# A graph network on Trainium2: windows of 128 nodes put in order of their number of edge tiles

## The chip, the cores and the metric

The kernel runs on one core of one Trainium2 chip. The metric is the device time of one execution in microseconds; the time shown is the median of 3 runs. The input is 6,250 nodes of 256 features and 100,000 edges sorted by destination; the destinations are drawn as 6250 u², so the first nodes have many edges and the last ones few.

## The reference

```python
x = layernorm(x + gcn(x, L0_W, edges))            # out[dst] += (x @ W)[src] * deg_inv_sqrt[src] * deg_inv_sqrt[dst]
y = x
for l in range(3):                                # 8 heads of 32
    Q, K, V = typed(y, W_Q[l]), typed(y, W_K[l]), typed(y, W_V[l])      # one of 4 matrices, by the node's type
    kt = typed(K[src], W_E[l], edge_type)                               # one of 3, by the edge's type
    s = sum(Q[dst] * kt, -1) / sqrt(32) * mu[l].T[edge_type]
    w = softmax of s over the edges with the same dst
    agg = segment_sum(V[src] * w, dst)
    y = layernorm(y + agg @ Wo[l] + bo[l]) * g1 + b1
    y = layernorm(y + gelu(y @ w1 + c1) @ w2 + c2) * g2 + b2
return layernorm(x + layernorm(y) * out_g + out_b)
```

## The kernel before

The nodes lie in `WINDOWS` = 50 windows of 128 (48 whole ones, window 48 with 106 nodes, window 49 empty). The edges of a window are cut into tiles of 128, and each window has at least one tile; a fixed `NT` = 832 tiles are worked on, two at a time (a duo), 16 tiles in a block. Tiles follow the windows in their order 0, 1, 2, ... The program is a row of stages, each a block of instructions for the five engines, with a barrier of all engines behind it (`end_phase`, L88), so that nothing of one stage runs beside another.

- `constants` (L137): masks, and the type of each node as a one-hot, `g.type_hot`. The types are loaded with one window in a row, turned by TensorE (L165), copied (L200) and compared (L203).
- `index_tiles` (L208): finds where each window's edges end (L450 to L462), the number of tiles of each window (`TILED`, L467), and by a running sum the tile at which each window starts (L468). From that it makes the window of each tile (`window_hot`, L476), gathers the edges of the tiles (POOL, L347, 7 gathers), counts the degree of each node (L513 to L531, then L388: the counts of the tiles summed into windows), and writes the tables of register words that steer the edge stages (L577 to L659). SyncE meanwhile copies x to SBUF (L321), and to `x_d`, the node state in DRAM (L323). The rows of x times 1/sqrt(degree) go to `xs_d` (L328).
- `gcn_edges` (L688): POOL gathers two times 128 rows of `xs_d` per duo (L764); TensorE multiplies them with a one-hot of the destinations into one of 4 PSUM banks, clears the next bank and ScalarE copies the bank of the window before to `g.sums`, for every tile, whether its window ended or not (L803 to L834). Which bank and which row is a word read into a register: `load_words` (L99), 16 or 24 words at once, each fourth duo.
- `gcn_nodes` (L1070): for windows two at a time (25 steps): the sums are scaled (L1155), turned (L1123), multiplied with W (L1132), added to x in `y` (L1235) and normalised. SyncE loads x in five batches of ten windows (L1105), then the weights of the projection (`load_weights`, L1295: `pj_wk` four times, `pj_we`, `pj_mu`, then eight parts of `pj_w`). TensorE turns the weights right after step n = 8 (`WEIGHTS_TURNED`; `turn_weights`, L1329, waits for all six of `k_in`). The new rows go to `x_d` and `x1_d` (L1113).
- The projection (`Projection`, L1260): for each of 49 windows, POOL spreads the rows by type (L1410), TensorE turns (L1346) and multiplies them (L1356), ScalarE and VectorE copy values, keys and query rows out, and SyncE stores keys and values in `kv_table` (`store_all`, L1307: two DMAs per window, each window at rows 128 n).
- `attention_edges` (L1477), three times: as `gcn_edges`, with gathers of `kv_table` (L1621), scores, softmax and weighted sums; also steered by words. `attention_nodes` (L1895), three times: output projection, layer norms and the feed-forward part for two windows at a time, with the next layer's projection behind it, in the last layer the final norms and the store of the result (L1991, one DMA per step).

SyncE's work stands in the order in which the code lists it: a DMA behind a wait or behind another DMA is issued after it.

```python
                for k in range(BATCHES):
                    some = batch_of(k)
                    sp.dma_start(y[:, some[0]:some[-1] + 1], windows_in(g.x_d, some)).then_inc(x_in[k], 16)
                pj.load_weights(sp)
```

Of the kernel before, what the change touches and what calls it, by code (L numbers as in the profile page):

```python
# [15 lines left out]
P = 128  # L16
# [36 lines left out]

FIRST_ROW, ZERO_ROW, UNREAD_ROW = ROWS, ROWS + 2, ROWS + 3
# [50 lines left out]

SUM_TOP = (SUM_BANK + SUM_BANKS - 1) * 512
# [30 lines left out]
def constants(nc, g):  # L137

    with ExitStack() as ctx:
        diff = ctx.enter_context(nc.sbuf_tensor("diff", [P, P], I32))  # L140
        type_rows = ctx.enter_context(nc.sbuf_tensor("type_rows", [WINDOWS, P], I32))
        type_rows_f = ctx.enter_context(nc.sbuf_tensor("type_rows_f", [WINDOWS, P], F32))
        type_col = ctx.enter_context(nc.sbuf_tensor("type_col", [P, WINDOWS], F32))
# [4 lines left out]
        turned = ctx.enter_context(nc.semaphore("const_turned"))  # L148
        whole = N // P
        with nc.Block() as block:  # L150
# [9 lines left out]

            @block.tensor
            def _(t):
                t.wait_ge(made, 6)
                t.wait_ge(masks, 3)
                t.transpose(g.ps[:, 0, 0:WINDOWS], type_rows_f[:], g.ident[0:WINDOWS, 0:WINDOWS]).then_inc(turned, 1)  # L165
# [19 lines left out]
            def _(v):  # L185
# [12 lines left out]
                v.tensor_copy(type_rows_f[:], type_rows[:]).then_inc(masks, 1)  # L198
                v.wait_ge(turned, 1)
                v.tensor_copy(type_col[:], g.ps[:, 0, 0:WINDOWS]).then_inc(masks, 1)  # L200
                v.wait_ge(masks, 4)
                for k in range(NODE_TYPES):
                    v.tensor_scalar(g.type_hot[:, :, k], type_col[:], float(k), None, ALU.is_equal)  # L203

        end_phase(nc, [made, masks, cleared, loaded, turned])


def index_tiles(nc, g):  # L208

    with ExitStack() as ctx:  # L210
# [3 lines left out]
        def sem(name):  # L214
# [25 lines left out]
        work = sb("ix_work", [P, 12, WINDOWS])  # L240
        ints = sb("ix_ints", [P, WINDOWS], I32)
# [37 lines left out]
            sem("ix_end_spread"))  # L279
        vec, base_ready, wdiag_ready, wrow_spread, wrow_copied = (  # L280
# [11 lines left out]
        K_COL, END_AT, DEG_AT = slice(0, 1), slice(64, 64 + WINDOWS), slice(128, 128 + WINDOWS)  # L292
# [7 lines left out]
        with nc.Block() as block:  # L300

            @block.sync
            def _(sp):
# [19 lines left out]
                sp.dma_start(g.x_d[0:N, :], g.x).then_inc(stored, 16)  # L323
                sp.dma_start(g.x_d[N:N + P, :], g.zeros[:, 0:D]).then_inc(stored, 16)
                sp.dma_start(g.x_d[N + P:NPAD, :], g.zeros[0:NPAD - N - P, 0:D]).then_inc(stored, 16)
# [25 lines left out]
            def _(t):  # L351
# [2014 lines left out]
```

## Time and profile before

| | us |
|---|---|
| time, median of 3 runs (lowest, highest) | 7778.57 (7768.23, 7786.26) |
| span of the profiled execution, first to last instruction | 6558.3 |
| the median less that span | 1220.3 |
| `constants` and `index_tiles` | 0 to 188 |
| `gcn_edges` | 188 to 1278 |
| `gcn_nodes` and first projection | 1278 to 1513 |
| `attention_edges`, three times | 1142, 1143, 1134 |
| `attention_nodes` with projection, twice | 580, 586 |
| last `attention_nodes` | 460 |

The profiled execution's own time is not among what is shown, only its span; the runs' median is 1220.3 us above that span. The bounds of the stages are read from the timeline, to a microsecond or two. SPq, PEldq, ACTq and DVEq are the sequencers of SyncE, TensorE, ScalarE and VectorE: rows of theirs are DMA issues and register instructions, which do not count as busy.

### The profile page before, as it was taken

How to read it: one execution, taken by the hardware profiler on the slowest of the kernel's cores; microseconds unless marked ns; L12 is line 12 of the kernel's file. 1: busy time of each engine (PE TensorE's matmuls, PEld its weight loads, DVE VectorE, ACT ScalarE, POOL GpSimd, SP SyncE). 2: the span in 40 equal slices, each digit the busy share in tenths (PEclk: the TensorE clock that was granted, in tenths of full speed). 3: DMA queues.
4: the chain of work that ended last, by engine and by line, in shares of the span. 5: the costliest groups of instructions: out<-in, count | busy, mean ns of one | idle time of the engine just before them, and what ended most of it. 6: DMA issues, size and time to landing. Idle time of an engine off the chain costs nothing. (4 is left out here: it accounts for less than half of the span.)

```text
span 6558.3 us, 128194 instructions
## 1 busy us (share of the span) xinstructions
PE 5376.9 (82%) x28010; PEld 4214.7 (64%) x28011; DVE 4522.3 (69%) x11029; ACT 3285.2 (50%) x10707; POOL 4047.3 (62%) x3930
## 2 busy tenths in 40 slices
PE   4566666697888888999888888889997888888897
PEld 3344444496666666788766666668896666666786
DVE  7433333356888888666488888876656888888697
ACT  0333333454666666323466666652244666666443
POOL 0677777546777777233577777743356777777343
PEclk9999999998999999999999999999998999999998
DMA  4444444578777777112887777741168777777111
GB/s 137 123 141 141 140 138 142 154 262 256 233 237 234 234 235 234 31 32 79 275 254 239 234 235 238 236 137 32 32 209 266 236 236 233 238 239 234 38 48 42
DMA packets 574994, 1165.93 MB, mean 178 GB/s; under 512 B 86616, under 2 KB 334128, under 8 KB 574752
## 3 DMA queue, kind: packets, MB, share of 16 engines
q0 software_dynamic: 239984, 774.78, 40.4%
q1 hardware_dynamic: 321359, 377.52, 17.5%
q10 hardware_dynamic: 13536, 12.33, 0.6%
q8 instruction: 44, 0.72, 0.0%
q14 instruction: 71, 0.57, 0.0%
HBM read 966.73 MB, written 204.00 MB: 179 GB/s over the span
## 5 line engine op out<-in xcount | busy, mean ns | idle before, releaser
L1621 POOL DMA_INDIRECT at_kv<-kv_table,at_stage x1664 | 1656.4, 995 | 545.0 <-issue 403.5
L1637 ACT COPY sums<-ps x2499 | 949.8, 380 | 1141.6 <-PE ps L1733 1116.8
L1718 PE MATMUL ps<-at_wv,at_hot 128*128 128x264 f32 x3328 | 1026.7, 403 | 348.5 <-ACT at_hot L1654 194.4
L1621 POOL DMA_INDIRECT at_kv_last<-kv_table,at_stage_last x832 | 824.7, 991 | 273.1 <-issue 205.4
L764 POOL DMA_INDIRECT gc_rows<-x_scaled,gc_stage x832 | 807.4, 970 | 269.9 <-issue 238.3
L1718 PEld LDWEIGHTS ps<-at_wv,at_hot 128*128 128x128 f32 x3328 | 515.1, 191 | 613.7 <-DVE at_wv L1820 354.4
L1733 PE MATMUL ps<-sums,at_hot_t 128*128 x3328 | 873.7, 386 | 26.7 <-DVE at_prod L1802 20.9
L825 PE MATMUL ps<-gc_rows,gc_hot 128*128 128x256 f32 x1664 | 552.4, 428 | 287.3 <-DMA gc_rows<-x_scaled,gc_stage 286.8
L1802 DVE TENSOR_TENSOR at_prod<-ps,at_kv 128x512 f32<-128x512 f32 x832 | 571.5, 687 | 285.5 <-DMA at_kv<-kv_table,at_stage 265.3
L1701 PE MATMUL ps<-zeros_b 128*128 128x264 bf16 x2508 | 695.8, 278 | 32.5 <-PEq L93 19.0
L1733 PEld LDWEIGHTS ps<-sums,at_hot_t 128*128 128x128 f32 x3328 | 579.2, 194 | 188.5 <-issue 19.9
L1718 PE MATMUL ps<-at_wv_last,at_hot_last 128*128 128x264 f32 x1664 | 508.7, 401 | 172.3 <-ACT at_hot_last L1654 111.9
L778 ACT COPY sums<-ps x833 | 310.9, 373 | 665.4 <-PE ps L825 649.8
L913 DVE CAST gc_hot_t<-ps 128x256 uint8<-128x256 f32 x416 | 176.3, 424 | 669.2 <-PE ps L825 665.3
L1843 DVE TENSOR_REDUCE at_score<-at_prod 128x16 f32<-128x512 f32 x832 | 563.8, 678 | 0.6
L825 PEld LDWEIGHTS ps<-gc_rows,gc_hot 128*128 128x128 f32 x1664 | 271.0, 205 | 425.2 <-DMA gc_rows<-x_scaled,gc_stage 367.9
L1820 DVE TENSOR_TENSOR at_wv<-at_kv,at_weight 128x462 f32<-128x462 f32 x832 | 526.7, 633 | 18.5 <-ACT at_weight L1674 5.2
L1684 ACT ACTIVATE at_wv<-at_kv,at_weight 128x33 f32<-128x33 f32 x1664 | 449.7, 323 | 3.4
L1718 PEld LDWEIGHTS ps<-at_wv_last,at_hot_last 128*128 128x128 f32 x1664 | 257.5, 190 | 301.8 <-DVE at_wv_last L1820 140.7
L1733 PE MATMUL ps<-sums,at_hot_t_last 128*128 x1664 | 437.8, 387 | 13.5 <-DVE at_prod_last L1802 10.2
L1802 DVE TENSOR_TENSOR at_prod_last<-ps,at_kv_last 128x512 f32<-128x512 f32 x416 | 285.8, 687 | 126.4 <-DMA at_kv_last<-kv_table,at_stage_last 124.2
L1666 ACT CAST at_hot_t<-at_hot_t 128x256 f32<-128x256 uint8 x832 | 345.4, 416 | 37.0 <-PE ps L1733 37.0
(411 smaller groups left out, 10812.2 us busy)
## 6 DMA issues: line engine op xcount, KB each, us to landing
kv_table<-pj_v_next SPq DMA_DIRECT2D x98, 396.0 KB, 3.5
kv_table<-pj_k_next SPq DMA_DIRECT2D x98, 384.0 KB, 2.8
at_hot_t<-hot_columns SPq DMA_DIRECT2D x104, 256.0 KB, 4.2
at_kv<-kv_table,at_stage POOLq DMA_INDIRECT x1664, 3.8
at_hot<-hot_rows SPq DMA_DIRECT2D x104, 256.0 KB, 4.8
at_rec<-block_records SPq DMA_DIRECT2D x104, 226.0 KB, 4.1
kv_table<-pj_v SPq DMA_DIRECT2D x49, 396.0 KB, 3.2
kv_table<-pj_k SPq DMA_DIRECT2D x49, 384.0 KB, 2.6
```

The source lines that it names most:

```text
L764: nc.gpsimd.indirect_dma_start(rows[:, (2 * k + j) * D:(2 * k + j + 1) * D], None, g.xs_d, bass.IndirectOffsetOnAxis(index, 0)).then_inc(g ...
L825: mm = t.matmul(at[j], hot[:, k, j, :], rows[:, (2 * k + j) * D:(2 * k + j + 1) * D], start=False, stop=True, skip_group_check=True)
L1621: nc.gpsimd.indirect_dma_start(kv[:, 2 * k + j, :], None, g.tab_d.rearrange("t n c -> (t n) c"), bass.IndirectOffsetOnAxis(index, 0)).then ...
L1637: act.copy(dest, source).then_inc(evacuated, 1)
L1666: act.copy(hot_t[:, slot % HRING].rearrange("p j e -> p (j e)"), hot_t8[:, b, u, :]).then_inc(t_cast, 1)
L1684: d = act.activation(wv[:, slot % WRING, j, SPLIT * UHEAD:UROW], kv[:, 2 * slot + j, D + SPLIT * UHEAD:SLOT], ACT.Copy, scale=weight[:, pa ...
L1701: return t.matmul(bank, g.zeros_b[:, 0:P], g.zeros_b[:], start=True, stop=True, skip_group_check=True)
L1718: mm = t.matmul(own[j], hot[:, slot % HRING, j, :], wv[:, slot % WRING, j, :], start=False, stop=True, skip_group_check=True)
L1733: mm = t.matmul(ps[:, TRIO[slot], j * D:(j + 1) * D], hot_t[:, slot % HRING, j, :], q_rows[j], start=True, stop=True)
L1802: v.tensor_tensor(prod[:, slot % 2].rearrange("p (j c) -> p j c", j=2), ps[:, TRIO[slot], :].rearrange("p (j c) -> p j c", j=2), keys, ALU ...
L1820: v.tensor_tensor(wv[:, slot % WRING, :, 0:SPLIT * UHEAD].rearrange("p j (h e) -> p j h e", h=SPLIT), kv[:, 2 * slot:2 * slot + 2, D:D + S ...
L1843: v.tensor_reduce(score[:, par, 2 * w:2 * w + 2, :], prod[:, slot % 2].rearrange("p (j h e) -> p j h e", j=2, h=HEADS), AX.X, ALU.add).the ...
```

## The change

The 48 whole windows are ranked by their number of tiles, fewest first (equal numbers by window); window 48 and the empty one keep their places at the end. Everything that was at window w is now at its rank: tiles, sums, query rows, state in DRAM, types. Sources of edges are still real node numbers, so `kv_table`, `xs_d` and the result stay in the order of the nodes, and what moves between the two orders looks up the real row. `g.window_rows` (one partition, 50 int32) holds the row of the window of each rank.

- `index_tiles` makes the order: a key of 64 tiles + window, its diagonal and a sum over it (L494 and L495 of the changed kernel), comparison with all other keys and a sum (the rank), a one-hot of the rank; TensorE multiplies ones with four rows of values times that one-hot, and the types with the one-hot, and VectorE copies both back. A second one-hot, by real window, is made for the degrees, and the degrees are summed twice (14 matmuls for 7).
- `constants` no longer turns the types; the four comparisons are made in `index_tiles`.
- x goes to a new DRAM tensor `x_padded`, and `gcn_nodes` loads it window by window.
- `store_all` looks up the row of each window before its wait; the result is stored with one DMA per window.

The diff, cut to its core:

```diff
+RANKED = N // P
+ORDER_LAST = 60000.0
+assert RANKED == FILLED - 1 == WINDOWS - 2 and (E // P + WINDOWS) * 64 + WINDOWS < ORDER_LAST
...
+def window_row(nc, g, eng, at):
+
+    _, (row,) = nc.values_load_multi_w_load_instructions(
+        g.window_rows[0:1, bass.ds(at, 1)], [eng.engine], skip_runtime_bounds_check_because=IN_RANGE)
+    return nc.s_assert_within(row, 0, RANKED * P, skip_runtime_bounds_check_because=IN_RANGE)
...
-                t.transpose(g.ps[:, 0, 0:WINDOWS], type_rows_f[:], g.ident[0:WINDOWS, 0:WINDOWS]).then_inc(turned, 1)
-                v.tensor_copy(type_rows_f[:], type_rows[:]).then_inc(masks, 1)
-                v.tensor_copy(type_col[:], g.ps[:, 0, 0:WINDOWS]).then_inc(masks, 1)
...
-                sp.dma_start(g.x_d[0:N, :], g.x).then_inc(stored, 16)
+                sp.dma_start(g.x_pad[0:N, :], g.x).then_inc(stored, 16)
+                sp.dma_start(g.x_d[FILLED * P:NPAD, :], g.zeros[:, 0:D]).then_inc(stored, 16)
...
+                t.wait_ge(ranks_ready, 1)
+                t.matmul(ps[:, 0, RANKS_AT], g.ones[:], by_rank[:].rearrange("p a w -> p (a w)"), start=True, stop=True)
+                t.matmul(ps[:, 0, TYPES_AT], g.type_rows_f[:], ranked[0:WINDOWS, :], start=True, stop=True).then_inc(ranks_spread, 1)
...
-                for c in range(CHUNKS):
-                    mm = t.matmul(ps[:, 0, DEG_AT], deg_rows[:, c * P:(c + 1) * P], window_hot[:, c, :],
-                                  start=c == 0, stop=c == CHUNKS - 1)
+                for k, hots in enumerate((window_hot, real_window_hot)):
+                    for c in range(CHUNKS):
+                        mm = t.matmul(ps[:, 0, 128 + k * WINDOWS:128 + (k + 1) * WINDOWS], deg_rows[:, c * P:(c + 1) * P], hots[:, c, :],
+                                      start=c == 0, stop=c == CHUNKS - 1)
...
+                v.tensor_copy(work[:, WINDOW], g.iota[:, 0:WINDOWS])
+                then(v.scalar_tensor_tensor(out=work[:, ORDER, 0:RANKED], in0=work[:, TILED, 0:RANKED], scalar=64.0,
+                                            in1=g.iota[:, 0:RANKED], op0=ALU.mult, op1=ALU.add))
+                then(v.tensor_tensor(diagonal[:], work[:, 0:5], g.ident[:, None, 0:WINDOWS].to_broadcast([P, 5, WINDOWS]), ALU.mult))
+                then(v.tensor_reduce(cols[:], diagonal[:], AX.X, ALU.add))
+                then(v.tensor_scalar(smaller[:], work[:, ORDER], cols[:, ORDER:ORDER + 1], None, ALU.is_lt))
+                then(v.tensor_reduce(rank_col[:], smaller[:], AX.X, ALU.add))
+                then(v.tensor_scalar(ranked[:], g.iota[:, 0:WINDOWS], rank_col[:], None, ALU.is_equal))
+                v.tensor_tensor(by_rank[:], ranked[:, None, :].to_broadcast([P, 4, WINDOWS]),
+                                cols[:, 0:4, None].to_broadcast([P, 4, WINDOWS]), ALU.mult).then_inc(ranks_ready, 1)
+                v.wait_ge(ranks_spread, 1)
+                v.tensor_copy(type_col[:], ps[:, 0, TYPES_AT])
+                then(v.tensor_copy(work[:, 0:4].rearrange("p a w -> p (a w)"), ps[:, 0, RANKS_AT]))
+                v.tensor_scalar(g.window_rows[:], work[0:1, WINDOW], float(P), None, ALU.mult)
...
+                then(v.tensor_tensor(mask[:], window_hot[:], work[:, WINDOW, None, :].to_broadcast(shape), ALU.mult))
+                then(v.tensor_reduce(tv[:, PAST], mask[:], AX.X, ALU.add))
+                v.tensor_tensor(real_window_hot[:], g.iota[:, None, 0:WINDOWS].to_broadcast(shape),
+                                tv[:, PAST, :, None].to_broadcast(shape), ALU.is_equal)
...
+                for k in range(NODE_TYPES):
+                    v.tensor_scalar(g.type_hot[:, :, k], type_col[:], float(k), None, ALU.is_equal)
...
-                DEG, SAFE, ROOT, HALF = 7, 8, 9, 10
+                DEG, SAFE, ROOT, HALF = (slice(8 + 2 * k, 10 + 2 * k) for k in range(4))
...
-                    sp.dma_start(y[:, some[0]:some[-1] + 1], windows_in(g.x_d, some)).then_inc(x_in[k], 16)
+                    for at in some:
+                        sp.dma_start(y[:, at, :], g.x_pad[bass.ds(window_row(nc, g, sp, at), P), :]).then_inc(x_in[k], 16)
...
-                    v.wait_ge(x_in[n // PER_BATCH], 16)
+                    v.wait_ge(x_in[n // PER_BATCH], 16 * len(batch_of(n // PER_BATCH)))
...
+                row = window_row(self.nc, g, sp, n)
                 sp.wait_ge(self.out_k, n + 1)
-                rows = g.tab_d[:, bass.ds(P * n, P), :].rearrange("t p c -> p t c")
+                rows = g.tab_d[:, bass.ds(row, P), :].rearrange("t p c -> p t c")
...
-                            sp.dma_start(two_windows(g.out, n - 5), fin[:, 1 - b]).then_inc(stored[1 - b], 16)
+                            for w in range(2):
+                                row = whole_window_row(nc, g, sp, 2 * (n - 5) + w)
+                                sp.dma_start(g.out[bass.ds(row, P), :], fin[:, 1 - b, w, :]).then_inc(stored[1 - b], 16)
```

Of how the change moves instructions, three places. SyncE in `gcn_nodes`, before:

```order
L1102 DMA gn_w<-in_L_gnn_W 128x2x256
L1105 DMA gn_y<-x_state 128x10x256 x4
L1105 DMA gn_y<-x_state 128x9x256
L1298 DMA pj_wk<-in_L_gnn_W_K 32x8x32 x4
L1299 DMA pj_we<-in_L_gnn_W_E 32x24x32
L1300 DMA pj_mu<-in_L_gnn_mu 128x24
```

and in the changed kernel, the last of the loads of x and the weights (an ISA row is an instruction without a name of its own in this listing; here it stands for the arithmetic on the register):

```order
L119 TENSOR_LOAD window_rows
L1149 ISA
L1149 DMA gn_y<-x_padded 128x256
L1342 DMA pj_wk<-in_L_gnn_W_K 32x8x32 x4
L1343 DMA pj_we<-in_L_gnn_W_E 32x24x32
L1344 DMA pj_mu<-in_L_gnn_mu 128x24
```

The first three rows stand there 49 times in a row, behind `gn_w` and ahead of the weights, where there were five DMAs.

VectorE in `index_tiles`, between the number of tiles and the running sum over it (listed as SCALAR_TENSOR_TENSOR ix_work<-ix_work,zeros), before:

```order
L465 TENSOR_SCALAR ix_ints<-ix_work 128x50
L466 TENSOR_SCALAR ix_ints<-ix_ints 128x50
L467 TENSOR_SCALAR ix_work<-ix_ints 128x50
L468 SCALAR_TENSOR_TENSOR ix_work<-ix_work,zeros 128x50
L469 TENSOR_TENSOR ix_work<-ix_work 128x50
```

and in the changed kernel:

```order
L489 TENSOR_SCALAR ix_work<-ix_ints 128x50
L491 COPY ix_work<-iota 128x50
L492 SCALAR_TENSOR_TENSOR ix_work<-ix_work,iota 128x48
L494 TENSOR_TENSOR ix_diagonal<-ix_work,ident 128x250
L495 TENSOR_REDUCE ix_cols<-ix_diagonal 128x5
L496 TENSOR_SCALAR ix_smaller<-ix_work,ix_cols 128x50
L497 TENSOR_REDUCE ix_rank_col<-ix_smaller 128x1
L498 TENSOR_SCALAR ix_ranked<-iota,ix_rank_col 128x50
L499 TENSOR_TENSOR ix_by_rank<-ix_ranked,ix_cols 128x200
L502 COPY ix_type_col<-ps 128x50
L503 COPY ix_work<-ps 128x200
L504 TENSOR_SCALAR window_rows<-ix_work 1x50
```

Eleven instructions stand between L489 and the sum, with two matmuls on TensorE between L499 and L502.

SyncE in the loop of `store_all`, changed kernel:

```order
L119 TENSOR_LOAD window_rows
L1358 REGISTER_ALU
L1360 ISA
L1360 DMA kv_table<-pj_k 128x3x256
L1361 ISA
L1361 DMA kv_table<-pj_v 128x3x264
```

The load of the row is new there; the two DMAs and their address arithmetic were there before. On POOL and ScalarE no instruction is added or moved.

## Rows read from the trace of the kernel before

**Rows 1.** The page: span of the profiled execution

```profile
span 6558.3 us, 128194 instructions
```

**Rows 2.** Busy time by stage: GCN edges, attention edges of one layer

```profile
core 0: us, PE busy (x) PEld busy (x) DVE busy (x) ACT busy (x) POOL busy (x), PEclk, DMA share, GB/s
...
188.00:1278.00 1090.00, 714.67 (x3384) 467.74 (x3384) 403.07 (x1276) 398.18 (x1249) 813.04 (x858) 0.95 0.46 139
...
1513.00:2655.00 1142.00, 949.40 (x4632) 699.94 (x4632) 916.35 (x1925) 727.61 (x2602) 837.70 (x858) 0.98 0.77 231
```

**Rows 3.** Timeline (start us, us, queue, line, DMA, count): SyncE, start of the GCN nodes

```profile
1279.43 11.59 SPq L1105 DMA_DIRECT2D gn_y<-x_state  x5
1291.07 5.88 SPq L1298 DMA_DIRECT2D pj_wk<-in_L_gnn_W_K  x4
...
1299.14 2.42 SPq L1300 DMA_DIRECT2D pj_mu<-in_L_gnn_mu  x1
```

**Rows 4.** Waits in 1278 to 1372 us (us in total, times, longest)

```profile
PE ps L1332 <- DMA pj_mu<-in_L_gnn_mu: 2.2, 1, 2.2
```

**Rows 5.** Source line of all register loads (count: ns min/median/max, first, last)

```profile
L101 PEldq TENSOR_LOAD <-words x324: 1612/1618/1665, 1513.7 to 6089.1; - x162
...
L101 DVEq TENSOR_LOAD <-words x156: 523/530/775, 1576.6 to 6088.6; - x156
...
L101 PEldq TENSOR_LOAD <-gcn_words x104: 1102/1107/1943, 188.6 to 1263.4; - x104
```

**Rows 6.** Timeline 1420 to 1433 us, projection of one window

```profile
1421.36 0.37 SPq L1315 DMA_DIRECT2D kv_table<-pj_k  x1
1421.92 0.37 SPq L1316 DMA_DIRECT2D kv_table<-pj_v  x1
...
1422.14 1.04 PE L1346 MATMUL ps<-ident,pj_xm 128*128 128x128 f32 x8
...
1424.40 0.37 SPq L1315 DMA_DIRECT2D kv_table<-pj_k  x1
```

**Rows 7.** Timeline 2650 to 2662 us, the same weight loads on an empty queue

```profile
2657.85 1.88 SPq L1298 DMA_DIRECT2D pj_wk_next<-in_L_gnn_W_K  x4
...
2660.41 0.39 SPq L1300 DMA_DIRECT2D pj_mu_next<-in_L_gnn_mu  x1
```

**Rows 8.** Source line L1300 (pj_mu), issue to landing

```profile
DMA to landing us min/median/max: 2.6/2.6/4.6
```

**Rows 9.** Timeline 1312 to 1372 us, TensorE after 8 us without work

```profile
1353.31 1.94 PE L1346 MATMUL ps<-ident,pj_xm 128*128 128x128 f32 x8 [7.76 <-ACT pj_xmt L1386]
```

**Rows 10.** Timeline 0 to 210 us, the two places of the index work

```profile
4.97 0.18 PEld L165 LDWEIGHTS ps<-ident,type_rows_f 50*128 50x128 f32 x1 [4.62 <-issue]
...
5.59 0.50 DVE L203 TENSOR_SCALAR type_hot<-type_col 128x50 f32<-128x50 f32 x4
...
27.10 0.67 PE L357 MATMUL ps<-ix_end_diag,ones 128*128 128x50 f32 x2 [10.03 <-DVE ix_end_diag L457]
...
29.73 0.21 DVE L470 SCALAR_TENSOR_TENSOR ix_work<-ix_work 128x50 f32<-128x50 f32 x1
29.86 0.52 DVE L471 TENSOR_TENSOR ix_mask<-ix_work,ix_tile_iota 128x350 f32<-128x350 f32 x1
...
51.51 9.29 DVE L500 COPY_PREDICATED ix_listed<-ix_shift_bits,ix_listed 128x1337 f32<-128x1337 int32 x7 [12.95 <-DMA ix_listed<-edge_pack,ix_base_row]
```

**Rows 11.** Timeline 136 to 150 us, degrees of the windows

```profile
137.41 3.23 PE L388 MATMUL ps<-ix_window_hot,ix_deg_rows 128*128 128x50 f32 x14 [1.06 <-ACT ix_deg_rows L407]
```

**Rows 12.** Busy time by stretch (columns as rows 2), index gathers and after a wait

```profile
30.00:51.00 21.00, 3.35 (x14) 3.06 (x14) 8.12 (x36) 0.00 (x0) 6.76 (x7) 1.00 1.09 372
...
1346.00:1360.00 14.00, 6.69 (x40) 6.72 (x41) 6.85 (x26) 5.23 (x10) 4.22 (x3) 0.63 1.02 340
```

**Rows 13.** Timeline, last node stage, SyncE: store and load of one step

```profile
6464.97 0.37 SPq L1974 DMA_DIRECT2D an_x_last<-x_state  x1
```

**Rows 14.** Timeline, last node stage, POOL: use of what that step loads

```profile
6480.92 1.26 POOL L2161 TENSOR_TENSOR an_xb_last<-an_x_last,nw_rows_last 128x512 f32<-128x512 f32 x1
```

More of the change, by code:

```diff
@@ L197, in _ @@
                 v.wait_ge(loaded, 32)
-                v.tensor_copy(type_rows_f[:], type_rows[:]).then_inc(masks, 1)
-                v.wait_ge(turned, 1)
-                v.tensor_copy(type_col[:], g.ps[:, 0, 0:WINDOWS]).then_inc(masks, 1)
[L201 to L205, printed above, removed]
+                v.tensor_copy(g.type_rows_f[:], type_rows[:])
+        end_phase(nc, [made, masks, cleared, loaded])
 def index_tiles(nc, g):
@@ L239, in index_tiles @@
         end_diag = sb("ix_end_diag", [P, WINDOWS])
-        work = sb("ix_work", [P, 12, WINDOWS])
-        ints = sb("ix_ints", [P, WINDOWS], I32)
+        work = sb("ix_work", [P, 16, WINDOWS])
+        ints = sb("ix_ints", [P, 2, WINDOWS], I32)
+        diagonal = sb("ix_diagonal", [P, 5, WINDOWS])
+        cols = sb("ix_cols", [P, 5])
+        smaller = sb("ix_smaller", [P, WINDOWS])
+        rank_col = sb("ix_rank_col", [P, 1])
+        ranked = sb("ix_ranked", [P, WINDOWS])
+        by_rank = sb("ix_by_rank", [P, 4, WINDOWS])
+        type_col = sb("ix_type_col", [P, WINDOWS])
+        real_window_hot = sb("ix_real_window_hot", [P, CHUNKS, WINDOWS])
         mask = sb("ix_mask", [P, CHUNKS, WINDOWS])
@@ L458, in _ @@
                 v.wait_ge(end_spread, 1)
-                END, START, COUNT, TILED, TEND, TST, OFF = range(7)
+                END, START, COUNT, TILED, ORDER, TEND, TST, OFF = range(8)
+                WINDOW = COUNT
                 v.memset(work[:, START, 0:1], 0.0)
+                v.memset(work[:, ORDER, RANKED:RANKED + 1], ORDER_LAST)
+                v.memset(work[:, ORDER, RANKED + 1:WINDOWS], ORDER_LAST + 1.0)
                 then(v.tensor_copy(work[:, END], ps[:, 0, END_AT]))
@@ L464, in _ @@
                 then(v.tensor_tensor(work[:, COUNT], work[:, END], work[:, START], ALU.subtract))
[L465 to L467 removed]
+                then(v.tensor_scalar(ints[:, 0], work[:, COUNT], float(P - 1), None, ALU.add))
+                then(v.tensor_single_scalar(ints[:, 0], ints[:, 0], 7, ALU.arith_shift_right))
+                then(v.tensor_scalar(work[:, TILED], ints[:, 0], 1.0, None, ALU.max))
+                v.tensor_copy(work[:, WINDOW], g.iota[:, 0:WINDOWS])
[12 more added lines that the diff above has]
+                v.tensor_scalar(g.window_rows[:], work[0:1, WINDOW], float(P), None, ALU.mult)
                 then(v.tensor_tensor_scan(work[:, TEND], work[:, TILED], g.zeros[:, 0:WINDOWS], 0.0, ALU.add, ALU.add))
@@ L539, in _ @@
                                        op1=ALU.add).then_inc(kv_ready, 1)
-                DEG, SAFE, ROOT, HALF = 7, 8, 9, 10
+                DEG, SAFE, ROOT, HALF = (slice(8 + 2 * k, 10 + 2 * k) for k in range(4))
                 v.wait_ge(deg_ready, 1)
-                then(v.tensor_copy(work[:, DEG], ps[:, 0, DEG_AT]))
+                then(v.tensor_copy(work[:, DEG].rearrange("p a w -> p (a w)"), ps[:, 0, DEG_AT]))
                 then(v.tensor_scalar(work[:, SAFE], work[:, DEG], 1.0, None, ALU.max))
@@ L2003, in _ @@
                     pj.store_all(sp)
-                sp.wait_ge(stored[0], 16 * ((STEPS + 1) // 2))
-                sp.wait_ge(stored[1], 16 * (STEPS // 2))
+                each = 32 if last else 16
+                sp.wait_ge(stored[0], each * (STEPS // 2) + 16)
+                sp.wait_ge(stored[1], each * (STEPS // 2))
             @block.tensor
@@ L2094, in emit @@
                         act.wait_ge(scaled, JOINT * n)
-                        need(act, stored[1 - b], 16 * (i - 3 + b))
+                        need(act, stored[1 - b], 32 * (i - 3 + b))
                         for k in range(2):
@@ L2333, in gnn_kernel @@
                 nc.sbuf_tensor("idx_x", [P, NT], I32) as g.idx_x:
+            constants(nc, g)
             index_tiles(nc, g)
```

36 lines of the change are left out of this document (17 added, 19 removed).

## The prediction

> **What bounds the kernel now.** I read the table of stages first, to see where the time is and what it depends on. The four edge stages hold most of it: 1090 us for the GCN and 1142 us for the edges of one layer [rows 2], of which there are three. Their instructions come from loops over 416 duos, whatever window a tile belongs to: each tile is gathered, multiplied, cleared and copied out in the same way, and the table words alone say which bank and row. So a new order of the windows changes words, not work, and I carry these stages over unchanged. What is left are the stages in which instructions are added: index, GCN nodes, projection, and the last node stage.
>
> Next, the timeline of SyncE at the start of the GCN nodes. Five loads of x keep its queue for 11.59 us, the weights follow, and `pj_mu` is issued at 1299.14 [rows 3] and lands 4.6 us later [rows 8]. The list of waits shows that TensorE stood 2.2 us for just that load [rows 4], with its matmul at 1303.8, right behind step 8 of 25. So **SyncE's queue is already on the path there**: whatever is put ahead of the weights moves the rest of the stage.
>
> **The change part by part.** *Loads of x in the GCN nodes.* Five DMAs become 49 times a register load, address arithmetic and a DMA of 128 rows. No register load of SyncE is in the trace. Three kinds of others are [rows 5]: 24 words on TensorE's queue 1618 ns, 16 words there 1107 ns, 2 words on VectorE's 530 ns. The two of TensorE lie on a line of 64 ns per word, which gives 0.15 us for one word; the upper bound is the 1.11 us of 16 words. I take 0.53 us, the row nearest in the number of words. Behind it come arithmetic and DMA: in the projection the second DMA starts 0.56 us after the first (1421.36, 1421.92) [rows 6], which holds both. One turn is 0.53 + 0.56 = 1.09 us, 49 are 53.4 us, against 11.59 us before. The Trainium skill, page "DMA: Bandwidth & Descriptors", section "Latency and other measured facts", puts a floor of about 600 ns under such a load; by it the turn were 1.16 us and the sum 3.4 us higher, but the 530 ns of VectorE's row lie below that floor.
>
> Part of this comes back. Before, the weights' issues stood in a full queue (5.88 us for the first four) [rows 3]; on an empty one the first to `pj_mu` takes 2660.41 - 2657.85 = 2.56 us, landing 2.6 us later [rows 7, 8]. With 128 KB per 1.09 us the queue will be nearly empty. So the weights are there at 1279.43 + 53.4 + 2.56 + 2.6 = 1338.0 instead of 1303.7: **34.3 us later**. The first eight steps need only two batches of x (20 turns, 21.8 us, and a landing), so they are done long before, and TensorE, ScalarE and VectorE then all stand, as their queues are in order and step 9 is behind the turned weights on TensorE. What follows them is the same work as before, by which the 34.3 us reach the end of the stage whole. ScalarE has no backlog it could work off in that time: its normalisations are listed seven steps behind the turned columns that it then waits for. The stores of x and of the table are behind the weights as before.
>
> *TensorE's restart.* After 8 us without work eight transposes took 1.94 us [rows 9], against 1.04 us in the steady loop [rows 6], in a stretch with a granted clock of 0.63 [rows 12], between its two levels of 1.2 and 2.4 GHz. It will now stand for some 30 us in the middle of the stage; for that and the matmuls right behind I add 2 us.
>
> *Index stage.* Between the number of tiles and the running sum stand seven new instructions in a chain, then two matmuls, then two copies. Ones of 50 columns take 0.21 us and those of 350 take 0.52 us [rows 10], with some 0.03 us between: five small ones 1.2 us, two of 250 columns 0.9, one of 200 and the copy of 200 0.8. The matmul of 50 columns (two passes) took 0.67 us [rows 10]; one of 200 and one of 50, with the signals there and back, I put at 1.4 us. Sum 4.3 us. From `constants` go a transpose, a copy and the four comparisons (4.97 to 6.09) [rows 10], 1.1 us; the comparisons come again, with the three of 350 columns for the second one-hot, where VectorE stands 12.95 us for the gathers [rows 10], and so cost nothing (2.1 us if that cover were gone). The degrees: seven matmuls took 3.23 us and VectorE waited for them [rows 11]; seven more are 3.2 us. Fourteen chained instructions on 100 instead of 50 columns add 0.05 us each, 0.7 us. Index: 4.3 - 1.1 + 3.2 + 0.7 = **7.1 us**. The gathers that then start 3.2 us later run in a stretch where the DMA engines are fully busy (share 1.09) with x [rows 12], so they could lose up to some 5 us more, or nothing; I take nothing and keep 5 us for the range. One DMA of zeros more is issued there beside them, at no cost.
>
> *Stores of keys and values.* A window takes 3.04 us (1421.36 to 1424.40) [rows 6], of which SyncE issues for 0.93 us. The register load stands ahead of its wait, so 0.53 us fall into 2.1 us of waiting, 147 times at no cost. Only a load above 2 us would be felt.
>
> *The result.* One more DMA and two register loads per step of 17 us. Behind them is the load of x, issued at 6464.97 [rows 13], landed some 3 us later, and used at 6480.92 [rows 14]: it may be 12 us late. Nothing there. Ahead of the last store, of which the code is unchanged, all is done.
>
> Sum: 34.3 + 2 + 7.1 = **43.4 us**. The profiled execution's span is 6558.3 us [rows 1], the median 7778.57 us, 1220.3 us more. I take what lies around the span as unchanged, so the span becomes 6601.7 us and the time 7822 us, 0.56% more. A measurement of this kernel can tell about 0.2%, 15.6 us, from no change.
>
> **The rivals.**
>
> *A: the register load is dear on SyncE.* At 1.11 us, as for 16 words, a turn is 1.67 us, 49 are 81.8, the weights land at 1366.4, 62.7 us later; with 9.1 us for the rest +72, 7850 us. For it: each queue has its own price in [rows 5], and SyncE's is not among them. Against: two words cost half. The Trainium skill, "Runtime: NRT & Kernel Launch", in its table of the preamble, has 1.3 us for the loads of a few words, from DRAM; by it the time were 7860 us. Chance 0.14.
>
> *B: it is cheap.* At 0.15 us a turn is 0.71 us, 49 are 34.8, the weights land at 1319.4, 15.7 us later: +25, 7803 us. For it: TensorE's two rows. Against: VectorE's lies 0.3 us above the same line. Chance 0.12.
>
> *C: it is hidden.* If the queue reads the register while the DMA ahead of it is issued, a turn is the 0.56 us of a DMA alone; 27.4 us, weights at 1312.0, 8.3 us later. TensorE then hardly stands, and with 7.1 us of index work the sum is +15, 7794 us: not slower by what can be measured. It decides from a turn of 0.56 us down. Against: the same queue issues one instruction after the other in [rows 3]. Chance 0.07.
>
> *D: the order itself moves the edge stages,* by reads and writes of banks and rows that meet otherwise. They are 1090 and, with the other layers about as long as the one of [rows 2], some 3420 us, so 1% is 45 us: enough to take the whole loss back (7777 us) or to double it (7867 us). For it only that the gathers' landing is what VectorE and TensorE wait for; against it that the sources, and with them the addresses gathered, are the same set. Chance 0.03 up and 0.04 down, half of the latter to below the time before.
>
> **How the numbers follow.** The forecast has 0.60: 7822 us, by itself 7812 to 7832 with the 5 us of the gathers and the runs' own spread of 9 us. A 0.14, B 0.12, C 0.07, D 0.07. The range reaches from B less that spread to A, 7797 to 7853 us, and leaves out C and D. Faster by over 0.2%: half of D's way down, 0.02. Within 0.2%: C and the other half, 0.09. Slower: 0.89.
>
> **What would show it.** In the changed profile: SyncE's register loads near 0.53 us, and 49 loads of x in 50 to 57 us; a wait of TensorE for `pj_mu` of some 30 us instead of 2.2; index stage 7 us longer; projection still 3.05 us per window; edge stages within a few us of before. I am wrong if TensorE does not wait there, if the projection loop has a longer period, or if an edge stage moved by over 10 us.

## The result, and the profile after

| | before | changed |
|---|---|---|
| median, us | 7778.57 | 7812.52 |
| lowest to highest, us (11 runs each) | 7743.28 to 7799.5 | 7791.03 to 7844.16 |
| ratio, 95% interval | | 1.0049 [1.0033, 1.0065] |

The changed kernel is slower by 0.49%, 34 us (by the interval 26 to 51 us). It was forecast at 7822 us, 43.4 us more.

One thing first, without which the numbers can't be read: the same kernel before took 6550 to 6559 us on the two chips of the first eight experiments, and 7760 us on that of the last two. The profile shown of before is of the first kind, the profile after of the second. Page of the changed kernel:

```profile
span 7789.3 us, 128925 instructions
```

Its profiled execution took 7791.03 us, 1.7 us more than its span. So the 1220.3 us between span and median of before [rows 1] do not lie around the span: they are another speed of the same program. Where they are is seen in the busy time by stretch. GCN edges, changed kernel (columns as in rows 2):

```profile
208.00:1496.00 1288.00, 799.47 (x3384) 536.55 (x3384) 394.47 (x1276) 398.80 (x1249) 809.82 (x858) 0.79 0.40 118
```

The same 3384 matmuls and 858 POOL instructions as in [rows 2], but 1288 us instead of 1090, with granted clock 0.79 instead of 0.95 and 118 GB/s instead of 139. The change does not do this: the kernel before has it too on such a chip (experiment 9).

The index stage and the node stage, where the change adds work, can be compared directly. SyncE at the start of the GCN nodes, changed kernel (timeline; columns as in rows 3):

```profile
1496.67 0.40 SPq L1145 DMA_DIRECT2D gn_w<-in_L_gnn_W  x1
1497.81 39.83 SPq L1149 DMA_DIRECT2D gn_y<-x_padded  x49
1537.69 1.90 SPq L1342 DMA_DIRECT2D pj_wk<-in_L_gnn_W_K  x4
1539.64 0.44 SPq L1343 DMA_DIRECT2D pj_we<-in_L_gnn_W_E  x1
1540.13 0.52 SPq L1344 DMA_DIRECT2D pj_mu<-in_L_gnn_mu  x1
```

Against [rows 3]: the loads of x keep the queue for 39.83 us where it was 11.59, and the weights behind them are issued in 2.44 us on a queue that is by then nearly empty. All register loads of a row, changed kernel (source line; columns as in rows 5):

```profile
L119 SPq TENSOR_LOAD <-window_rows x196: 261/604/921, 1497.1 to 5843.3; - x196
```

The row mixes two kinds. The 49 loads ahead of the weights (the same line, 1497 to 1538 us) are the short ones:

```profile
L119 SPq TENSOR_LOAD <-window_rows x49: 261/269/507, 1497.1 to 1536.9; - x49
```

The 49 of each of the three projections have medians of 619, 670 and 701 ns. In the straight run the turns are 0.81 us apart (39.83 / 49), and with 0.27 us for the load some 0.54 us remain for arithmetic and DMA. Waits in the node stage, changed kernel:

```profile
PE ps L1377 <- DMA pj_mu<-in_L_gnn_mu: 23.7, 1, 23.7
ACT pj_wkt L1425 <- PE ps L1377: 22.5, 1, 22.5
DVE gn_y L1279 <- DMA gn_y<-x_padded: 15.9, 1, 15.9
```

TensorE waits 23.7 us for the last weight load, where it was 2.2 [rows 4], and ScalarE with it. VectorE's 15.9 us for the first ten windows of x are new too; they end before TensorE's wait does and cost nothing. TensorE on both sides of its wait (timeline):

```profile
1517.26 1.89 PE L1176 MATMUL ps<-gn_w,gn_at 128*128 128x256 f32 x8
1542.85 1.89 PE L1377 MATMUL ps<-ident,pj_wk 128*32 128x128 f32 x8 [23.70 <-DMA pj_mu<-in_L_gnn_mu]
1544.54 1.06 PE L1167 MATMUL ps<-ident,gn_a 128*128 128x128 f32 x4
1545.39 2.77 PE L1176 MATMUL ps<-gn_w,gn_at 128*128 128x256 f32 x8
1548.00 0.60 PE L1167 MATMUL ps<-ident,gn_a 128*128 128x128 f32 x4
```

and before:

```profile
1303.80 1.05 PE L1332 MATMUL ps<-ident,pj_wk 128*32 128x128 f32 x8 [2.25 <-DMA pj_mu<-in_L_gnn_mu]
1304.69 0.60 PE L1123 MATMUL ps<-ident,gn_a 128*128 128x128 f32 x4
1305.12 1.89 PE L1132 MATMUL ps<-gn_w,gn_at 128*128 128x256 f32 x8
```

The three groups behind the wait take 5.7 instead of 3.5 us: 2.2 us for the restart. The granted clock of these stretches:

```profile
1520.00:1543.00 23.00, 0.15 (x1) 0.13 (x2) 2.00 (x6) 2.28 (x6) 3.75 (x2) 0.57 0.57 151
1543.00:1550.00 7.00, 7.00 (x32) 5.79 (x30) 1.35 (x3) 4.63 (x10) 0.00 (x0) 0.70 0.16 25
1550.00:1560.00 10.00, 10.00 (x62) 8.80 (x61) 8.99 (x38) 8.11 (x19) 0.00 (x0) 1.00 0.38 125
```

While TensorE stands, the granted clock is 0.57, near the lower of its two levels (1.2 of 2.4 GHz); it is 0.70 in the stretch behind the wait and 1.00 in the next. The node stage closes to a tenth with these numbers. From the issue of `gn_w` to TensorE's restart it was 1303.80 - 1279.0 = 24.8 us and is 1542.85 - 1496.7 = 46.2, so 21.4 us more; with 2.2 for the restart 23.6. From `gn_w` to the first store of keys it was 81.2 us (1279.0 to 1360.2), and is 104.9 (1496.7 to 1601.6): 23.7 us more.

Index stage, changed kernel, VectorE from the number of tiles to the running sum, and the gathers (timeline, columns as in rows 10):

```profile
27.60 0.19 DVE L489 TENSOR_SCALAR ix_work<-ix_ints 128x50 f32<-128x50 int32 x1
...
31.96 0.21 DVE L502 COPY ix_type_col<-ps 128x50 f32<-128x50 f32 x1 [1.72 <-PE ps L375]
...
32.58 0.24 DVE L505 TENSOR_TENSOR_SCAN ix_work<-ix_work,zeros 128x50 f32<-128x50 f32 x1
...
67.19 5.63 DVE L543 COPY_PREDICATED ix_listed<-ix_shift_bits,ix_listed 128x1337 f32<-128x1337 int32 x4 [23.36 <-DMA ix_listed<-edge_pack,ix_base_row]
```

The ranks take 4.8 us (27.8 to 32.6; 4.3 were forecast), and the chain ahead of them is 1.4 us shorter (its matmul starts at 25.7 instead of 27.1; 1.1 were forecast). But the wait for the gathers has grown from 12.95 us [rows 10] to 23.36, and what follows starts at 67.2 instead of 51.5. The second set of degree matmuls, right behind the first:

```profile
153.28 3.23 PE L407 MATMUL ps<-ix_window_hot,ix_deg_rows 128*128 128x50 f32 x14 [1.06 <-ACT ix_deg_rows L426]
156.31 3.19 PE L407 MATMUL ps<-ix_real_window_hot,ix_deg_rows 128*128 128x50 f32 x14
```

That is the 3.2 us of the forecast. The projection is unchanged: stores of keys at 1604.75 and 1607.80, 3.05 us apart, against 3.04 [rows 6].

### The profile page after: what moved, and what is told of

Its sections match the earlier page's. It is cut to its first block and busy times, and to the rows that moved or that the text cites. A ratio compares the mean times of both kernels' runs of the same rounds, so it can differ in the third digit from the quotient of the medians.

```text
span 7789.3 us, 128925 instructions
## 1 busy us (share of the span) xinstructions
PE 5917.6 (76%) x28027; PEld 4501.4 (58%) x28028; DVE 4504.7 (58%) x11044; ACT 3289.5 (42%) x10707; POOL 4068.3 (52%) x3930
## 5 line engine op out<-in xcount | busy, mean ns | idle before, releaser
L1763 PE MATMUL ps<-at_wv,at_hot 128*128 128x264 f32 x3328 | 1119.5, 432 | 339.8 <-DVE at_wv L1865 154.5
L1746 PE MATMUL ps<-zeros_b 128*128 128x264 bf16 x2508 | 746.4, 298 | 523.8 <-ACT sums L1682 253.7
L1778 PE MATMUL ps<-sums,at_hot_t 128*128 x3328 | 1000.8, 429 | 45.8 <-DVE at_prod L1847 21.2
L1763 PEld LDWEIGHTS ps<-at_wv,at_hot 128*128 128x128 f32 x3328 | 572.3, 208 | 626.7 <-issue 289.0
L1778 PEld LDWEIGHTS ps<-sums,at_hot_t 128*128 128x128 f32 x3328 | 647.5, 216 | 229.2 <-issue 68.4
L1746 PEld LDWEIGHTS ps<-zeros_b 128*128 128x128 bf16 x2508 | 261.6, 104 | 742.1 <-issue 346.0
L1763 PE MATMUL ps<-at_wv_last,at_hot_last 128*128 128x264 f32 x1664 | 563.1, 434 | 167.1 <-DVE at_wv_last L1865 73.2
L868 PE MATMUL ps<-gc_rows,gc_hot 128*128 128x256 f32 x1664 | 616.5, 469 | 2.9 <-DMA gc_rows<-x_scaled,gc_stage 2.9
L850 PE MATMUL ps<-zeros_b 128*128 128x256 bf16 x836 | 273.8, 328 | 437.0 <-ACT sums L821 300.7
L1778 PE MATMUL ps<-sums,at_hot_t_last 128*128 x1664 | 498.2, 427 | 22.5 <-issue 14.4
```

The costliest lines, as they stand in the source:

```text
L868: mm = t.matmul(at[j], hot[:, k, j, :], rows[:, (2 * k + j) * D:(2 * k + j + 1) * D], start=False, stop=True, skip_group_check=True)
L1746: return t.matmul(bank, g.zeros_b[:, 0:P], g.zeros_b[:], start=True, stop=True, skip_group_check=True)
L1763: mm = t.matmul(own[j], hot[:, slot % HRING, j, :], wv[:, slot % WRING, j, :], start=False, stop=True, skip_group_check=True)
L1778: mm = t.matmul(ps[:, TRIO[slot], j * D:(j + 1) * D], hot_t[:, slot % HRING, j, :], q_rows[j], start=True, stop=True)
```

## The experiments

After the result two things had to be explained: the index stage had lost more than twice the 7.1 us of its term, and the loads of x had cost less than theirs. My theory of the index stage: the gathers come to stand behind the copy of all of x (6.4 MB), which SyncE issues at the same time. The rivals: the gathers merely start later and the copy has no part in it; or the new order of the windows moves the edge stages (rival D) and the sums only look right. Ratios are to runs of the kernel before on the same chip.

**1. The kernel before, again** (no edit).

> The kernel before once more, unchanged, for a profile on the same chip as the others. The profile of the changed kernel has a span 1.7 us below its time, so this one should have a span of about 7775 us too, not 6558, and its edge stages should be about as long as those of the changed kernel (1288 us for the GCN). If the order of the windows were what made them long, they would be near 1090 and 1142 us here. Ratio to before 1.000.

Measured: ratio 0.9998 [0.9989, 1.0007], 6557.66 us, span 6557.2 us. The expected span was wrong: on this chip the kernel itself takes 6558 us, and the profiled execution 6558.96, 1.8 us more than its span. The stage times of the next experiments are set beside this profile; experiments 5 to 8 ran on another chip, so their medians are compared with the kernel before there. How much a stage varies with nothing changed is seen in the end of the index stage: 188.6 us in the profile of [rows 1], 191.4 here, 191.9 in experiment 5. VectorE goes on behind the gathers at 51.5, 54.2 and 54.5 us in these three.

**2. The changed kernel, again** (no edit).

> The changed kernel once more, unchanged. By my theory its stages differ from those of the kernel before, profiled on the same chip, by about 10 to 20 us in the index stage (7 us of added work and the later gathers) and about 20 to 25 us in the GCN nodes, and by nothing beyond the scatter of runs in the edge stages. Ratio 1.004 to 1.006. By the rival, in which the order moves the edge stages, those differ by more than 10 us in sum.

Measured: 1.0066 [1.0052, 1.0079], a little above what was expected; medians 6601.41 and 6558.66 us: 42.8 us. In the two profiles of one chip each stage can be set beside the other (start of GCN edges is the clearing of `br_last_key`; nodes are from `gn_w`'s issue to the first store of keys; projection from there to the clearing of `at_ends_max`):

| us | index ends | GCN edges | GCN nodes | projection |
|---|---|---|---|---|
| before (1) | 191.4 | 1091.7 | 82.1 | 153.6 |
| changed (2) | 207.5 | 1091.4 | 104.0 | 153.1 |
| difference | +16.1 | -0.3 | +21.9 | -0.5 |

The two terms make 38.0 us. The medians differ by 42.8 and the two spans by 33.1 (6590.3 - 6557.2), so some 5 us either way are the spread of single executions, and no stage is named for them. Attention edges and nodes of the first two layers took 1731.6 and 1712.0 us before, 1728.5 and 1715.0 with the change, the last layer 1594.8 and 1590.8: none moved by over 4 us. VectorE at its wait for the gathers, kernel before, and then changed:

```profile
54.19 9.29 DVE L500 COPY_PREDICATED ix_listed<-ix_shift_bits,ix_listed 128x1337 f32<-128x1337 int32 x7 [15.60 <-DMA ix_listed<-edge_pack,ix_base_row]
```

```profile
66.83 5.63 DVE L543 COPY_PREDICATED ix_listed<-ix_shift_bits,ix_listed 128x1337 f32<-128x1337 int32 x4 [22.86 <-DMA ix_listed<-edge_pack,ix_base_row]
```

12.6 us later, although the first gather was issued only 3.4 us later (34.2, 37.6). Landing of the gathers from their issue, before and then changed:

```profile
DMA to landing us min/median/max: 5.7/5.9/12.3
```

```profile
DMA to landing us min/median/max: 5.2/18.0/21.3
```

**3. Ranks by window number alone**: all the added work, but the order of before.

```diff
-  ... in0=work[:, TILED, 0:RANKED], scalar=64.0,
+  ... in0=work[:, TILED, 0:RANKED], scalar=0.0,
```

> All added work is kept, but the key of a window is its number alone, so that every window keeps its place. My theory (the added instructions cost, the order does not): ratio 1.004 to 1.006, as the changed kernel. Rival (the order moves the edge stages): the ratio moves away from that of the changed kernel by more than 0.2%.

Measured: 1.0061 [1.0047, 1.0074], the index stage ends at 207.8, TensorE waits 23.1 us for `pj_mu`. As the changed kernel: the order itself does nothing that can be told (0.05% between the two ratios), the work around it costs the rest. Rival D, 1% of the edge stages, is out.

**4. The weights ahead of the 49 loads of x**, in the changed kernel.

```diff
+                pj.load_weights(sp)
                 for k in range(BATCHES):
...
-                pj.load_weights(sp)
```

> The weights' DMAs stand ahead of the 49 loads of x. My theory: TensorE no longer waits some 24 us for pj_mu behind step 8; instead the first batch of x is some 6 us later. The GCN node stage gets 14 to 20 us shorter than in the changed kernel, ratio about 1.002 to 1.004. If the 49 loads themselves were the limit (x of a step later than its matmuls), the stage would stay as long.

Measured: 1.0031 [1.0018, 1.0043]; 23 us of the 43 come back in the medians (6601.41 to 6578.33), 17.4 of them in the node stage; the rest is within the spread of single executions seen in experiment 2. The node stage is 86.6 us (1298.8 to 1385.4) instead of 104.0, TensorE's wait for `pj_mu` is gone, and VectorE waits for its first ten windows instead:

```profile
DVE gn_y L1279 <- DMA gn_y<-x_padded: 21.9, 1, 21.9
```

So the added node time is the wait for the weights behind the loads, as forecast. What is left of it (4.5 us) is that first batch: TensorE in turn waits for VectorE to free a bank, which it did not do in the kernel before.

```profile
PE ps L1176 <- DVE gn_y L1279: 3.7, 1, 3.7
```

**5. The kernel before with 49 loads of x at fixed addresses**: the DMAs of the change without its register loads.

```diff
-                    sp.dma_start(y[:, some[0]:some[-1] + 1], windows_in(g.x_d, some)).then_inc(x_in[k], 16)
+                    for at in some:
+                        sp.dma_start(y[:, at, :], g.x_d[at * P:(at + 1) * P, :]).then_inc(x_in[k], 16)
```

> The kernel before with its five loads of x (node stage of the GCN) cut into 49 loads of one window each, at fixed addresses: as many DMAs as the changed kernel, none of its register loads. If the number of DMAs carries the later weights, 49 of them take over 30 us and pj_mu is waited for by TensorE for over 10 us, ratio 1.003 or more. If the register load and its arithmetic carry it (0.81 us per turn, of which 0.26 are the load), a fixed turn is 0.40 to 0.55 us, the 49 take 20 to 27 us instead of 11.6, the weights on an emptier queue take back 4 to 8 us of that, TensorE waits for pj_mu no longer than 10 us, and the ratio is 0.9995 to 1.001.

Measured: 1.0014 [1.0005, 1.0023].

```profile
1281.22 24.50 SPq L1106 DMA_DIRECT2D gn_y<-x_state  x49
```

A fixed turn is 0.50 us (24.50 / 49), one with a register load 0.81. TensorE waits 8.9 us for `pj_mu`, inside what was expected, and the node stage is 90.9 us, 8.8 more than before; the ratio is above the 1.001 that I had as the upper end. So the number of DMAs carries about 8.8 of the 21.9 us, and register loads with their arithmetic the other 13 (the profiles compared are of two chips).

**6. The changed kernel without the copy of x**: the node stage loads x from the input.

```diff
-                sp.dma_start(g.x_pad[0:N, :], g.x).then_inc(stored, 16)
+                sp.dma_start(g.x_pad[whole * P:N, :], g.x[whole * P:N, :]).then_inc(stored, 16)
...
-                        sp.dma_start(y[:, at, :], g.x_pad[bass.ds(window_row(nc, g, sp, at), P), :]).then_inc(x_in[k], 16)
+                        rows = g.x[bass.ds(whole_window_row(nc, g, sp, at), P), :] if at < RANKED else g.x_pad[RANKED * P:FILLED * P, :]
+                        sp.dma_start(y[:, at, :], rows).then_inc(x_in[k], 16)
```

> The changed kernel without the copy of x to x_padded (only its last 106 rows are copied); the node stage loads x from the input, in the same order and with the same register loads. If the copy is what the gathers of the edges stand behind, they land in 6 us or less, VectorE's wait for them falls from 22.9 to below 14 us, the index stage ends 8 to 13 us earlier than in the changed kernel (GCN edges start at 195 to 200 instead of 207.5) and the ratio to the kernel before is 1.004 to 1.0055. If the gathers are slow by themselves or for the loads of x to SBUF, they start at 205 or later and the ratio stays at 1.0061 to 1.007. The node stage should be as in the changed kernel, 22 us longer than before, in either case.

Measured: 1.0035 [1.0023, 1.0047].

```profile
DMA to landing us min/median/max: 3.7/4.0/4.9
...
49.26 3.08 DVE L543 COPY_PREDICATED ix_listed<-ix_shift_bits,ix_listed 128x1337 f32<-128x1337 int32 x2 [5.43 <-DMA ix_listed<-edge_pack,ix_base_row]
```

The gathers, issued at 37.6 as in the changed kernel, land after 4.0 us instead of 18.0; VectorE waits 5.4 us instead of 22.9; the index stage ends at 190.2 instead of 207.5, 17.3 us, more than the 8 to 13 us I had expected, and the ratio is below the 1.004 that I had as the lower end. The node stage is 105.3 us, about as in 2. The copy is what the gathers stand behind. The chips differ between this run and 2, but the index stage does not follow the chip: it ends at 207.3 to 208.2 us in four profiles with the copy in its place, and at 189.7 to 190.2 in three where it is not there (6, 7, 10), over three chips.

**7. Both: no copy, and the weights first**, in the changed kernel.

> Both at once: no copy of x in the index stage, and the weights issued ahead of the 49 loads of x. If the two places are all that the change costs, their gains add: GCN edges start at 195 to 200, the node stage is 4 to 6 us longer than before instead of 22, and the ratio is 1.0010 to 1.0025. If something else carries part of the cost, the ratio stays above 1.003.

Measured: 1.0009 [1.0000, 1.0018]. Index ends at 189.9 (195 to 200 were expected), nodes take 87.1 us (+5.0). The gains add: of 43 us about 5 remain by the medians, and by the interval 0 to 12.

**8. The same two edits in the kernel before.**

> The kernel before with the same two edits (no copy of x in the index stage, the weights ahead of its five loads of x). Its gathers already landed in 5.9 us and its weights were waited for by 2.2 us only, so little is to be had: if the copy costs this kernel nothing, the ratio is 0.9995 to 1.0005; if the copy delays its gathers too, or the stage after it, up to 10 us come back and the ratio is 0.998 to 0.9992. The node stage then waits for its first batch of x instead, about 5 us.

Measured: 0.9991 [0.9982, 1.0000]; index ends at 184.9 instead of 191.4, nodes take 81.7 us. The kernel before paid for the copy too: 6.5 us, or 7.0 against experiment 5 on the same chip, though only 3.7 against the profile of [rows 1]. The difference of 7 and 8 is the change in its cheapest form: 5.0 us in the index stage (189.9 - 184.9) and 5.4 us of nodes. The 5.0 us are not all of the added work. The gathers of 7 are issued 3.4 us later than those of 8 (37.6 and 34.2), but VectorE goes on only 1.5 us later (49.12 and 47.65), since they land after 4.1 us instead of 5.9 (medians); behind them 3.5 us are added. So the work is 3.4 + 3.5 = 6.9 us, against 7.1 of the forecast, and 1.9 of it lie under the wait. By the medians, 6547.22 us, this is the fastest of the kernels measured on that chip, but the interval reaches to no change.

**9. The kernel before with its gathers 3.4 us later**: one instruction of 50 columns made 16 times.

```diff
-                then(v.tensor_scalar(work[:, TILED], ints[:], 1.0, None, ALU.max))
+                for _ in range(16):
+                    then(v.tensor_scalar(work[:, TILED], ints[:], 1.0, None, ALU.max))
```

> The kernel before with one 50-column instruction of the index chain repeated 15 times more, so that its gathers are issued 3.5 to 4.5 us later (near 38.2 us instead of 34.2), and nothing else. If the gathers lose time because they come to stand behind the copy of x (issued at 39.0 here), the loss is more than the delay: landing of the later gathers 12 us or more instead of 5.9, the copy instruction on VectorE that waits for them starts 8 to 12 us later than 54.2, GCN edges start at 200 to 204 instead of 191.4, ratio 1.001 to 1.002. If a delay only adds itself, they start at 195 to 196 and the ratio is 1.0003 to 1.001.

Measured (on a chip where before takes 7759.61 us): 1.0011 [0.9996, 1.0027].

```profile
66.43 4.39 DVE L501 COPY_PREDICATED ix_listed<-ix_shift_bits,ix_listed 128x1337 f32<-128x1337 int32 x3 [24.55 <-DMA ix_listed<-edge_pack,ix_base_row]
```

The gathers are issued at 37.6 instead of 34.2, and VectorE goes on at 66.4 instead of 54.2: a delay of 3.4 us has become 12.2, about what the change lost there (12.6), and the index stage ends at 203.2, 11.8 us later. The copy is issued at 38.84 us, as before (38.97 in experiment 1); then four of the seven gathers were issued ahead of it, here one. The ratio alone would not have told this; its interval holds no change. The GCN edges took 1290.6 us here (203.2 to 1493.8), as in the changed kernel's profile on such a chip, so they do not come from the change.

**10. The changed kernel with the copy kept whole, but issued when the gathers have landed**, and the weights first.

```diff
+                sp.wait_ge(listed_in, 16 * CHUNKS)
                 sp.dma_start(g.x_pad[0:N, :], g.x).then_inc(stored, 16)
```

> The changed kernel with the copy of x to x_padded kept whole, but issued when the gathers have landed (near 49 us), and the weights ahead of the loads of x. If the copy costs only by its place ahead of the gathers, this is as good as leaving it out: GCN edges start at 189 to 192, the node stage is 5 to 7 us longer than before, ratio 1.0005 to 1.002. If the copy costs wherever it stands (for instance by delaying the end of the stage or the edge stage's first gathers), GCN edges start at 197 or later and the ratio is 1.002 or more.

Measured: 1.0008 [0.9995, 1.0020], on the chip of 9. The gathers' wait is 4.9 us, the copy is issued at 48.93, the index stage ends at 189.7, nodes take 86.7 us (4.6 longer than in 1; 5 to 7 were expected). The copy costs by its place, not by its bytes: in experiment 6 the DMA engines had nothing to do behind the gathers, and here they carry the copy in that time, with VectorE as busy as there. Busy time by stretch, experiment 6 and then 10 (columns as in rows 2):

```profile
50.00:60.00 10.00, 0.00 (x0) 0.00 (x0) 9.72 (x9) 0.00 (x0) 0.00 (x0) 1.00 0.00 0
```

```profile
50.00:60.00 10.00, 0.00 (x0) 0.00 (x0) 9.71 (x9) 0.00 (x0) 0.00 (x0) 0.50 1.06 350
```

## Why the prediction was right, and where it was not

*The bound.* Right: SyncE's queue ahead of the weights was on the path, and TensorE's wait for `pj_mu` is where the added time of the node stage shows (23.7 us). Experiment 4 takes it away by moving the weights and nothing else.

*Loads of x, 34.3 us.* Mis-sized. The step that failed is "I take 0.53 us, the row nearest in the number of words": in the straight run a load took 0.27 us, half of it. The other part of a turn, 0.56 us, held (0.54), and so did the weights on an empty queue, 2.56 us (2.44) and 2.6 us to the landing (2.7). With 0.81 us per turn the term came out as 21.4 us, between the forecast and rival B (15.7 us at 0.15 us a load), nearer to B. The two bounds, 0.15 and 1.11 us, held it. In the loops of the projections the same load takes 0.6 to 0.7 us, where it costs nothing. The Trainium skill, page "DMA: Bandwidth & Descriptors", section "Latency and other measured facts", has about 600 ns as a floor: the loads in the loops have medians near it (619 to 701 ns), those of the straight run lie well below (269 ns), and the measurement decides.

*TensorE's restart, 2 us.* Right: 2.2 us.

*Index stage, 7.1 us.* The work was sized well: ranks 4.8 for 4.3, what falls away in `constants` 1.4 for 1.1, degrees 3.2 for 3.2, and experiments 7 and 8 give 6.9 us in all. The step that failed is "they could lose up to some 5 us more, or nothing; I take nothing": the gathers lost 9.2 us on top of their own delay (12.6 less 3.4), and the stage 16.1 us. The row had been read ([rows 12], share 1.09), but only as a number of busy engines; what was not asked is what the 6.4 MB behind the loads of x do to gathers that are issued behind them. Before, the copy is issued at 39.0, behind the fourth of the seven gathers (34.2 to 41.8); in the changed kernel at 37.7, with the first of them (37.6 to 45.2).

*The sum.* On one chip, 16.1 + 21.9 = 38.0 us for the forecast 43.4, which is two misses that offset each other: -12.9 us in the loads (21.4 for 34.3) and +9.0 in the index stage. That the forecast total lay inside the result's interval of 26 to 51 us is in part luck.

*The range.* Its bounds do not follow from its own words: B less the spread of 9 us is 7794 us and not 7797, and 7853 us is 3 us above A. The measured 7812.5 us lies inside either way.

*The time around the span.* Wrong: "I take what lies around the span as unchanged" treated 1220.3 us as time outside the program, and it is the program at another speed. It did no harm, since the added pieces take the same microseconds at both: 22.9 and 23.4 us of wait for the gathers, 22.3 and 23.7 for `pj_mu`, index ending at 207.5 and 208.2. They are issue times and waits for DMAs, not long matmul loops.

*Costed at nothing.* Right: the projection's period (3.05 us), the result's stores (the last layer is 4.0 us shorter in experiment 2 than in 1), the edge stages, the one-hot made under the gathers' wait.

*The rivals.* A is out (a load costs a quarter of its 1.11 us). B is nearer than the forecast for the loads of x (15.7 and 34.3 us, measured 21.4), but its total of +25 us took the index term as it was forecast, too. C is out: with the register load a turn is 0.81 us, without it 0.50 (experiment 5). D is out by experiment 3.

## What to carry to other kernels

A run of small DMAs ahead of something that is waited for costs most of the issue time that it adds: here 28.2 us more of issue cost 21.4. Put the awaited load first, and what stays is the wait for the first batch (4.5 us here). Look at what a gather that is waited for is issued beside: here 3.4 us of earlier work cost 12.2, because more of the gathers then stood behind a large copy, and holding the copy back until they had landed brought back 17 us of the index stage. And compare the profiled span with the time of its own execution before treating the rest as overhead; where only medians of other runs are given, the gap may be another speed of the machine.

## What the runs showed of the hardware

- A register load of one word on SyncE takes 0.27 us or 0.6 to 0.7 us (medians), by place. The loads of the projections have the second; the straight run of the GCN nodes and those of the last node stage, changed kernel, the first:

```profile
L112 SPq TENSOR_LOAD <-window_rows x48: 262/268/471, 7409.8 to 7779.1; - x48
```

  What decides between the two was not tried.
- Two speeds of one program: 6550 to 6559 us and 7760 to 7779 us, by the chip. The edge stages carry it (GCN edges 1090 and 1288 us), while index, GCN nodes and projection are within 1 us at both (nodes 104.0 and 104.9 us, projection 153.1 and 153.6). The lower granted clock there (0.79 for 0.95) is not all of it: in the GCN edges the same matmuls keep TensorE busy for 85 us more (799.47 for 714.67), and the stage is 198 us longer. The rest is standing. In the longest stand TensorE, VectorE and ScalarE have next to no work while POOL goes on issuing gathers, with the clock at its lower level and the DMA engines a third busy (changed kernel, profile of the result, columns as in rows 2):

```profile
237.70:258.30 20.60, 2.38 (x7) 1.29 (x6) 0.24 (x1) 0.00 (x0) 15.21 (x18) 0.50 0.35 99
```

  ScalarE's wait that ends there is 20.7 us; the longest that it has in this stage in experiment 2 is 4.8. This speaks for gathers that land late as the first cause, but what the engines wait for is not named in that trace, so it is not shown.
- Seven gathers of 128 rows, issued by POOL, land after 4.0 us (median) with no copy beside them, 5.9 (the last 12.3) when four are issued ahead of it, 18.0 when it is issued with the first. In experiment 2 VectorE's wait ended at 66.8 us, and the DMA engines were busy to about 62 (busy time by stretch, columns as in rows 2):

```profile
50.00:60.00 10.00, 0.00 (x0) 0.00 (x0) 0.00 (x0) 0.00 (x0) 0.00 (x0) 1.00 1.03 334
60.00:64.00 4.00, 0.00 (x0) 0.00 (x0) 0.00 (x0) 0.00 (x0) 0.00 (x0) 1.00 0.59 181
64.00:66.00 2.00, 0.00 (x0) 0.00 (x0) 0.00 (x0) 0.00 (x0) 0.00 (x0) 1.00 0.14 57
```

  So the last gather landed when the DMA engines were all but through with what was queued, the copy last. The Trainium skill, page "DMA: Bandwidth & Descriptors", section "Queues, rings and completion order", says that a DMA engine takes turns between its queues, a packet at a time; if the turns were even in bytes, gathers of 0.92 MB would not have lasted as long as the 6.4 MB. How large the turns of either were, no run here shows.
